# Graph network chain on Trainium2: a message gather in 128-column products, packed control words and stored one-hots

## The reference

```python
# message network, 3 layers
m = concatenate([x[src], x[dst], ew], -1)            # 103125 edges x (64 + 64 + 1)
m = relu(m @ edge_W[l] + edge_b[l])
agg = segment_sum(m, dst, n)
x = relu(concatenate([x, agg], -1) @ node_W[l] + node_b[l])
# relation network
h0 = relu(x @ W_enc + b_enc)
agg = segment_sum(einsum('nd,rdo->rno', h0, W_rel)[etypes, src], dst, n)
# sage network, 2 passes
agg = segment_sum(h[src], dst, n) / max(deg, 1)
# attention network, 2 layers: edge softmax over 2 heads, 3 power steps each
```

## Time and profile before

| what | value |
|---|---|
| median of 3 runs | 13450.17 us (13437.72 to 13457.99) |
| the profiled execution, from its first to its last instruction | 13453.0 us |
| message layer 0 | 843 us |
| message layers 1 and 2, each | 779 us |
| relation pass | 1215 us |
| sage passes | 561 and 562 us |
| attention network, from the end of the sage passes on | about 6310 us |
| TensorE busy over the whole span | 83% |
| VectorE busy over the whole span | 81% |

### The profile page before, as it was taken

The page is one execution under the profiler, slowest core; times in us unless marked ns, Lnnn a source line. Parts: engine busy times, 40 slices in busy tenths (PEclk is TensorE's granted clock), DMA queues, the critical chain, the costliest instruction groups (busy, mean ns, idle before and its releaser), DMA issues. The chain is left out here.

```text
span 13453.0 us, 456368 instructions
## 1 busy us (share of the span) xinstructions
PE 11137.4 (83%) x106911; PEld 9882.7 (73%) x106912; DVE 10911.2 (81%) x40164; ACT 5227.5 (39%) x19100; POOL 2409.1 (18%) x7659
## 2 busy tenths in 40 slices
PE   3555399899899599976665879999998789999998
PEld 3444388799798499975553339999997338999998
DVE  6545399688688288876565999999997999999998
ACT  1000022122222022235452338865453337875454
POOL 2777300000000000001110001112221001222222
PEclk9999999899899599999896999999998999999999
DMA  1111177444243011113231554432221554432222
GB/s 54 47 50 47 45 228 236 138 128 128 80 128 115 4 41 41 41 50 88 71 87 51 148 140 115 115 92 73 70 73 47 143 147 113 115 98 73 70 73 61
DMA packets 1206840, 1232.94 MB, mean 92 GB/s; under 512 B 218352, under 2 KB 1042801, under 8 KB 1206107
## 3 DMA queue, kind: packets, MB, share of 16 engines
q1 hardware_dynamic: 1180954, 1228.47, 32.8%
q0 software_dynamic: 25792, 3.35, 0.2%
HBM read 1115.06 MB, written 116.16 MB: 92 GB/s over the span
## 5 line engine op out<-in xcount | busy, mean ns | idle before, releaser
L993 DVE TENSOR_SCALAR hot<-iota_row,place 128x128 f32<-128x128 f16 (+1 forms) x9000 | 1818.8, 269 | 158.5 <-PE acc L1092 135.7
L1711 ACT ACTIVATE msgs<-G,share 128x64 f32<-128x64 f32 x6000 | 1395.6, 315 | 1346.0 <-PE G L1725 1346.0
L985 DVE TENSOR_SCALAR hotT<-idx,iota_col 128x512 bf16<-128x512 f16 x4500 | 1323.8, 352 | 524.4 <-PE G L1138 492.1
L1725 PE MATMUL G<-u_b,hotT 128*128 x12000 | 1592.2, 276 | 50.3 <-DVE hotT L1659 50.3
L1735 PE MATMUL S<-msgs,hot 128*128 128x128 f32 x12000 | 1586.3, 275 | 0.0
L1157 ACT CAST msgs<-G 128x384 bf16<-128x384 f32 x2250 | 1020.4, 480 | 1372.7 <-PE G L1138 1368.1
L1725 PEld LDWEIGHTS G<-u_b,hotT 128*128 128x128 f32 x12000 | 1467.4, 193 | 51.0 <-issue 51.0
L1735 PEld LDWEIGHTS S<-msgs,hot 128*128 128x128 f32 x12000 | 1462.3, 192 | 0.0
L1080 PE MATMUL G<-table_m,hotT 128*128 x9000 | 1309.8, 248 | 93.4 <-issue 69.3
L1110 ACT ACTIVATE msgs<-sums 128x128 f32<-128x128 f32 x2250 | 699.3, 311 | 1762.3 <-DVE sums L1102 1400.5
L1547 ACT ACTIVATE msgs<-G,msgs 128x64 f32<-128x64 f32 x6000 | 1315.5, 333 | 30.5 <-issue 21.0
(11 more groups left out here) (323 smaller groups left out, 19877.9 us busy)
## 6 DMA issues: line engine op xcount, KB each, us to landing
idx<-pos_rows SPq DMA_DIRECT2D x6375, 128.0 KB, 2.9
hotT<-hots_d SPq DMA_DIRECT2D x750, 256.0 KB
hots_d<-hotT SPq DMA_DIRECT2D x375, 256.0 KB, 3.4
key_b<-key_rows SPq DMA_DIRECT2D x62, 416.0 KB
ty_b<-type_rows SPq DMA_DIRECT2D x62, 416.0 KB
rows<-rel_rows SPq DMA_DIRECT2D x1500, 6.0 KB
ew_now<-ew_rows_d SPq DMA_DIRECT2D x1125, 3.0 KB
sorted_d<-recs,place POOLq DMA_INDIRECT x806
```

What stands on the lines that cost most here:

```text
L985: op = eng.tensor_scalar(hotT[:, c % deep, n], idx[:, c, r], p.col[:, first:first + 1], None, ALU.is_equal)
L993: op = eng.tensor_scalar(hot[:, c % 2, q], p.row16[:], place[:, c % 2, q:q + 1], None, ALU.is_equal)
L1711: op = eng.activation(msgs[:, c % 2, 2 + j // HEADS, j % HEADS * D:(j % HEADS + 1) * D], G[c % 2][1][:, j * D:(j + 1) * D], ACT.Copy, scal ...
L1725: mm = eng.matmul(G[c % 2][b][:, k * W:(k + 1) * W], hotT[:, c % 2, q * P:(q + 1) * P], table[:, ds(dst_at(at, q, 24 * W), W)], start=True ...
```

## The change

**Message layers.** The tables have four planes of 25 x 64 columns (high, middle, zeros, low part), and one product reads two planes: 128 columns as 2 x 64. For each chunk the sender and the receiver take two products each, planes 0 and 1 and then 2 and 3, into the same 128 PSUM columns, and the edge weight takes one of 64 columns with nine rows instead of three. ACT copies one of the two halves (`half`), DVE adds the other (`add`), ACT takes the relu, and DVE and POOL work out what is left over after the upper 16 bits of each message (`remains`, `lowest`). The scatter has three bf16 products of 64 columns for each chunk that read the upper halves of those fp32 values; the degree takes a product of 2 columns in layer 0. TensorE gathers quarter t and scatters quarter t-3.

**Words.** One word for each quarter holds the source block and four destination blocks of 5 bits. TensorE loads 8 to 11 words once for every eight quarters, and takes a block from a word with a shift and a remainder.

**One-hots.** Layer 0 builds all three kinds and stores them for pairs of quarters (768 KB). Layers 1 and 2 load two kinds and build the third. The relation pass loads the scatter one-hot (built before) and builds the gather ones. The sage passes load both, and ACT and DVE share the cast. SP's loads are for two quarters each.

**Set-up.** The edge weights' rows are written out nine times instead of three.

```diff
-WIDE, FIVE = 102, 5
-LAST = 4 * 512 + 4 * WIDE
+PAIRS = (QUARTERS + 1) // 2
+KINDS = 3
+LAST = (BLK - 1) * D
...
-                for i in range(EW):
+                for i in range(EW_ROWS):
...
+                chain(eng, v, [lambda: eng.tensor_copy(upper[0:1], four[:, :, 3:4])]
+                      + [lambda c=c: eng.scalar_tensor_tensor(upper[0:1], upper[0:1], 32.0, four[:, :, c:c + 1], ALU.mult, ALU.add)
+                         for c in (2, 1, 0)]
+                      + [lambda: eng.tensor_copy(one, upper[0:1]),
+                         lambda: eng.tensor_copy(upper_i[0:1], lead),
+                         lambda: eng.tensor_scalar(upper_i[0:1], upper_i[0:1], 20, None, ALU.logical_shift_left),
+                         lambda: eng.tensor_tensor(one, one, upper_i[0:1], ALU.bitwise_or)])
...
+def load_packed(p, eng, t, count):
+
+    of = p.ctl[0:1, ds(t, count)]
+    _, words = p.nc.values_load_multi_w_load_instructions(
+        of, [eng.engine], min_val=0, max_val=WORD,
+        skip_runtime_bounds_check_because="the table is computed here from block numbers that are clamped to 0..24")
+    return words
+
+
+def dst_block(word, q, times=D):
+
+    return (((word >> 5 * q) if q else word) % 32 * times).with_bounds(min_val=0, max_val=(BLK - 1) * times)
+
+
+def src_block(word, times=D):
+
+    return ((word >> 20) * times).with_bounds(min_val=0, max_val=(BLK - 1) * times)
+
...
+def tensor_turns(p, eng, step, lag):
+
+
+    words = load_packed(p, eng, 0, 8)
+    for t in range(8):
+        step(t, t, words[t], words[t - lag] if t >= lag else None)
+    with eng.Fori(1, QUARTERS // 8) as i:
+        words = load_packed(p, eng, i * 8 - lag, 8 + lag)
+        for c in range(8):
+            step(i * 8 + c, c, words[c + lag], words[c])
...
+                def lowest(t, c):
+                    ready(eng, lefted, t + 1)
+                    eng.tensor_tensor(msgs[:, c % 4, 2], msgs[:, c % 4, 1], upper[:, c % 4, 1], ALU.subtract
+                                      ).then_inc(made.h, 1)
...
+                def add(t, c):
+                    ready(eng, halved, t + 1)
+                    ready(eng, relud, t + 1)
+                    eng.tensor_tensor(sums[:, c % 4], both(c)[:, :, 0], half[:, c % 4], ALU.add).then_inc(added.h, 1)
+
+                def remains(t, c):
+                    ready(eng, relud, t + 5)
+                    eng.tensor_tensor(msgs[:, c % 4, 1], msgs[:, c % 4, 0], upper[:, c % 4, 0], ALU.subtract
+                                      ).then_inc(lefted.h, 1)
...
+                    if not make:
+                        eng.dma_start(hots[:, c:c + n, 0:2].rearrange("p k n e -> p k (n e)"),
+                                      s.hots_d[ds(pair, 1), :, 0:n, 0:2 * 4 * P].rearrange("o p k e -> (o p) k e")
+                                      ).then_inc(idx_in[c // 2].h, 16)
...
+                def gather(t, c, at):
+                    ready(eng, turned, t + 1)
+                    ready(eng, added, t - 3)
+                    of = src_block(at)
+                    for q in range(4):
+                        to = G[c % 4][:, q * 2 * D:(q + 1) * 2 * D]
+                        for side in range(2):
+                            hot = hots[:, c, 1 + side, q * P:(q + 1) * P]
+                            table = s.table3[side][:, :, ds(dst_block(at, q) if side else of, D)]
+                            eng.matmul(to.rearrange("p (i f) -> p i f", f=D), hot, table[:, 0:2],
+                                       start=(side == 0), stop=False, skip_group_check=True)
+                            eng.matmul(to.rearrange("p (i f) -> p i f", f=D), hot, table[:, 2:4],
+                                       start=False, stop=False, skip_group_check=True)
+                        mm = eng.matmul(to[:, 0:D], s.ew_now[:, c, q * P:(q + 1) * P], s.we9[:, l], start=False, stop=True,
+                                        skip_group_check=True)
+                    mm.then_inc(gathered.h, 1)
+
+                def scatter(t, c, was):
+                    ready(eng, made, t + LAG + 1)
+                    for q in range(4):
+                        hot = hots[:, c, 0, q * P:(q + 1) * P]
+                        if degrees:
+                            eng.matmul(acc[:, BLK * D:BLK * (D + 2)][:, ds(dst_block(was, q, 2), 2)],
+                                       hot, p.onesb[:], start=False, stop=False, skip_group_check=True)
+                        to = acc[:, ds(dst_block(was, q), D)]
+                        for part in range(3):
+                            mm = eng.matmul(to, hot, upper[:, c % 4, part, q], start=False, stop=False, skip_group_check=True)
+                    mm.then_inc(scattered.h, 1)
...
+                def gather(t, c, h, at):
+                    of = src_block(at)
+                    for k in range(2):
+                        q = 2 * h + k
+                        for r in range(NT):
+                            mm = eng.matmul(G[c % 2 * 2 + h][:, k * 3 * D:(k + 1) * 3 * D].rearrange("p (q f) -> p q f", f=D),
+                                            hotT[:, c % DEEP, r, q * P:(q + 1) * P] if make else hot[:, c, 1, q * P:(q + 1) * P],
+                                            tables[r][:, :, ds(of, D)], start=(r == 0), stop=(r == NT - 1))
+                    mm.then_inc(gathered[h].h, 1)
+
+                def scatter(t, c, h, was):
+                    for k in range(2):
+                        q = 2 * h + k
+                        to = acc[:, ds(dst_block(was, q), D)]
+                        for part in range(3):
+                            mm = eng.matmul(to, hot[:, c, 0, q * P:(q + 1) * P],
+                                            msgs[:, c % 4, q, part], start=False, stop=False, skip_group_check=True)
+                    return mm
...
-        def gather(eng, c, h, at, env):
-            for k in range(2):
-                q = 2 * h + k
-                for side in range(2):
-                    mm = eng.matmul(env["G"][h][:, k * 3 * D:(k + 1) * 3 * D],
-                                    env["hotT"][:, c % env["deep"], side, q * P:(q + 1) * P],
-                                    s.table3[side][:, ds(dst_at(at, q, LAST) * 2 if side else src_at(at, 24 * 3 * D), 3 * D)],
-                                    start=(side == 0), stop=False)
-                mm = eng.matmul(env["G"][h][:, k * 3 * D:(k + 1) * 3 * D], s.ew_now[:, c, q * P:(q + 1) * P],
-                                s.we3[:, l].rearrange("p q f -> p (q f)"), start=False, stop=True)
-            return mm
-
-        def scatter(eng, c, h, at, env):
-            j = (2 * (c - 1) + h) % 4
-            for k in range(2):
-                q = 2 * h + k
-                mm = eng.matmul(env["acc"][:, ds(dst_at(at, q, LAST), WIDE)], env["hot"][:, (c - 1) % 2, q, :], msgs[:, j, k, :],
-                                start=False, stop=False, skip_group_check=True)
-            return mm
...
-        s.table3 = [p.sb("table_m0", [P, BLK * 3 * D], BF16, ctx), p.sb("table_m1", [P, 2 * FIVE * 512], BF16, ctx)]
+        s.table3 = [p.sb(f"table_m{i}", [P, 4, BLK * D], BF16, ctx) for i in range(2)]
...
-        s.hots_d = p.dram("hots_d", [QUARTERS, P, 2 * 4 * P], BF16)
-        s.ew_rows = p.dram("ew_rows_d", [EW, CHUNKS * P], BF16)
+        s.hots_d = p.dram("hots_d", [PAIRS, P, 2, KINDS * 4 * P], BF16)
+        s.ew_rows = p.dram("ew_rows_d", [EW_ROWS, CHUNKS * P], BF16)
```

More of the change, by code:

```diff
@@ L33 @@
 EW = 3
+EW_ROWS = EW * EW
 RELS, RELS_BIG, HEADS, LAYERS = 8, 500, 2, 2
@@ new lines, in eights, with first_uses, ready, quarters_in @@
+def eights(eng, step):
+    for t in range(8):
+        step(t, t, t // 2)
+    with eng.Fori(1, QUARTERS // 8) as i:
+        for c in range(8):
+            step(i * 8 + c, c, i * 4 + c // 2)
+    for t in range(QUARTERS // 8 * 8, QUARTERS):
+        step(t, t % 8, t // 2)
+def first_uses(t, c, each):
+    return each * (t // 8) if isinstance(t, int) else (t - c) * (each // 8)
+def ready(eng, sem, count):
+    if not isinstance(count, int) or count > 0:
+        after(eng, sem, count)
+def quarters_in(t):
+    return 1 if isinstance(t, int) and t == QUARTERS - 1 else 2
@@ L963, in _, with store @@
-                quarters(eng, step)
-                if keep == "store":
-                    for t in range(Q - 4, Q):
-                        store(t, t % 4)
-                    for c in range(4):
-                        eng.wait_ge(stored[c].h, 16 * ((Q - c + 3) // 4))
+                def store(t, c, pair, n):
+                    ready(eng, made, t + n + LAG)
+                    eng.dma_start(s.hots_d[ds(pair, 1), :, 0:n].rearrange("o p k e -> p (o k e)"),
+                                  hots[:, c:c + n].rearrange("p k n e -> p (k n e)")).then_inc(stored[c // 2].h, 16)
@@ L970, in _ @@
+                eights(eng, step)
+                if make:
+                    for t in range((Q - 1) // 2 * 2 - 2, Q, 2):
+                        store(t, t % 8, t // 2, quarters_in(t))
```

(37 more changed lines are left out.)

424 lines of the change are left out of this document (209 added, 215 removed).

## The result

The changed kernel takes 15044.12 us in the median of 4 runs (15036.43 to 15063.28), the kernel before 13452.14; the ratio is 1.119 with an interval of 1.117 to 1.120. It is slower, as forecast, but by 1592 us where 778 were forecast, and outside the range (13,940 to 14,510). The profiled execution has a span of 15049.6 us.

What follows compares the result with a forecast made beforehand. TensorE's queue of address entries, word loads and products was taken as the bound. Layer 0 +427, layers 1 and 2 +576, relation -75, sage -160 and set-up +10 sum to +778: 14,230 us, range 13,940 to 14,510.

Steps and rivals of the forecast that it cites:

- The queue as the bound: TensorE's queue of addresses, word loads and products bounds message layers 1 and 2: 2.85 us a quarter against 2.08.
- the factor: Queue sums are multiplied by 1.025, from a sage quarter before: sum 1.46 us, measured 1.50.
- Scatter: 100+78 and 3 x 210: 808: Message layers 1 and 2: the scatter's four address entries with their products take 808 ns of queue a quarter.
- Shift and remainder: Address entries on TensorE's queue: both surcharges count in full, so an entry with both takes 132 ns.
- Rival C: Address entries: the shift is free beside the remainder, six entries at 98 ns; 13,920 us, chance 0.06.
- The load of words: TensorE's queue, once in eight quarters: 11 words take 788 ns, about 830 with what stands behind.
- the ring: Layer 0, not forecast: a store's wait on SP's queue holds back the next loads; two quarters take 9 us.
- Layer 0's stores: Layer 0: stores grow from 256 to 384 KB a quarter, but the DMAs' share, 0.61, stays hidden.
- Relation and sage: Cheaper word loads, and in sage a shorter queue, give back 75 us in relation and 80 in each sage pass.
- A: Message layers: the array bounds, not the queue, so layers 1 and 2 take 1.40 us a quarter; 12,550 us, chance 0.08.
- B: Address entries: shift and remainder cost nothing beyond a plain entry, 0.65 us less a quarter; 13,230 us, chance 0.03.
- D: Message layers: waits between engines add 1.11 times to the queue sum again, +280 us; 14,510 us, chance 0.13.

Runs made afterwards that it cites:

- aligned words: Changed kernel with each load of packed words starting four words before the group and taking 12 words; 14540.45 us, 1.087 of the kernel before.
- remainder only: On the kernel with both repairs, blocks are remainders by 25, 24, 23 and 22 of the word, without a shift; 13958.83 us, 1.037 of the kernel before.
- both repairs: Changed kernel with the aligned 12-word load and layer 0's store one pair of quarters later; 14137.25 us, 1.057 of the kernel before.
- late store: Changed kernel with only layer 0's store of the one-hots issued one pair of quarters later; 14665.78 us, 1.097 of the kernel before.
- one address a side: On the kernel with both repairs, the gather goes back to one product of 192 columns a side; 13545.48 us, 1.006 of the kernel before.
- shared addresses: On the kernel with both repairs, all four chunks of a quarter use the first one's destination block; 13050.41 us, 0.975 of the kernel before.

## Why the prediction was wrong in size, and where its mechanism held

**The queue as the bound** held. Edits that touch TensorE's entries and loads alone moved layer 1 by what they took off the queue: 83 us of queue for 82 of pass (aligned words) and 73.0 for 73.1 (remainder only). The size of the sum held in part by luck. Its 2.78 us a quarter, 2.85 with the factor, is 2.71 in the kernel with both repairs, but the term "Scatter: 100+78 and 3 x 210: 808" holds in three of eight quarters only. In the other five the entries are plain and the same rule gives 2 x 42 + 2 x 37 + 4 x 78 = 470 ns, so the mean is 597, 0.21 us less, 79 us a pass. The sum would have been 2.57, and the measured time 1.05 times that; a term too dear and a factor too small met halfway.

**Shift and remainder**: 132 taken for both in one entry, 131 to 141 measured in the gather and a median of 126 in sage; a remainder alone 88 to 94. So the surcharges do add up. Rival C (the shift free) would have been 98.

**The load of words** is the first step that failed: "11 words (593-334 is 65 for a word, so 593 + 3 x 65 = 788, about 830 with what stands behind)". It took 2637 ns. All loads of the kernel before start at a multiple of four words and take a multiple of four, and I carried their price over to one that starts three or two words ahead of such a place. By 2637, 2402 and 850 ns for 11 and 10 words off it and 12 on it, a word costs about 235 there and 65 here; 11 words on it, at 1326, lie between. It took 82 us in each of layers 1 and 2 and 84 in layer 0 (1367 to 1283, once the ring was gone), 115 in the relation pass and 84 and 87 in sage: 534 us, which turned +778 into about +1312 and the gains of the relation and sage passes into losses.

In layer 0 the load has a second price that I can't explain. The kernel with the late store and the one with both repairs, in layer 0:

```profile
L897 PEldq TENSOR_LOAD <-ctl x46: 3591/3843/4160, 1640.2 to 2952.7; - x46
```

```profile
L897 PEldq TENSOR_LOAD <-ctl x45: 857/2030/2369, 1639.3 to 2842.3; - x45
```

That is 1.2 us more than the same loads take in layer 1, 55 us over the pass, and part of why layer 0 comes to 1283 although its scatter was taken too dear as well (1336 ns a quarter, where the trace's entries and the same rule give 1155). Nearly all of these loads stand 1.4 to 1.6 us behind the issue of a store; in the kernel with one address a side they stand 3.6 to 4.1 us behind it and take 850 ns. But the kernel with the late store has one 7.4 us behind, at 3862 ns, so the place alone doesn't explain it, and no run tests a cause.

**Layer 0's stores** are the second step that failed: "0.73 x 640/512 x 2.25/3.39 is 0.61, so they hide". The bytes did hide; the wait ahead of them did not. I costed the store as traffic and never asked what stands behind its wait on SP's queue. Undone, layer 0 fell by 411 us with the load aligned (1694 to 1283), and by 323 without. The two misses together are 853 us by the passes and 832 by the ratios (1.119 to 1.057); the forecast missed by 814.

**The array** at 128 columns was taken at 56 ns, halfway between two rows, and the timeline of the kernel with shared addresses, where no queue holds it up, shows that:

```profile
3000.30 0.22 PE L1146 MATMUL G<-table_m,hots 128*128 x1
3000.30 0.10 PEld L1148 LDWEIGHTS G<-table_m,hots 128*128 128x128 bf16 x1
3000.36 0.22 PE L1148 MATMUL G<-table_m,hots 128*128 x1
...
3001.31 0.52 PE L1163 MATMUL acc<-msgs,hots 128*128 128x64 bf16 x12
```

Between 3000.30 and 3001.31 lies the gather of one quarter, 16 products of 128 columns and four of 64: 1.01 us, and 16 x 56 + 4 x 29 is 1.01. The Trainium skill's 81 ns for a sustained pair of weight load and product at 128 columns ("TensorE: Matmul & The Clock Gate", "Back-to-back issue gap") is not what this kernel shows; the formula of the same section, 56 ns, which it gives for a single product, fits.

**Hidden work**: POOL's subtraction, given 0.3 to 1.4 us, took 0.615; DVE's additions, 0.35 to 0.52, took 0.42. Both were hidden; DVE in layer 0, given 55 to 65% of the span, has 38% in the kernel after and 53% with both repairs (677 of 1270 us). **Relation and sage** would have gained what was forecast within 31 and 20 us, once the load was aligned. **Set-up**: layer 0 starts at 1688 us before and 1692 after, where 10 more were forecast, but this stretch differs by more between the groups of runs, so that term is open.

**The rivals**: A's mechanism failed, and its price too: with nine of fourteen entries gone the message layers stop at 1.95 us a quarter, at loads. B and C are refuted by the entries' durations, 131 to 141 ns where B had 48 and C 98. D, slower still by 280 us, had the side of the miss but a third of its size, and named neither cause.

## What to carry to other kernels

Price an instruction from a row with the same alignment as well as the same size: a load into registers that started off a 16-byte place cost more than three times as much for each word, and 11 words cost more than 12 from the same kind of start. Read the queue's entries in every step of an unrolled loop, since some of them may be worked out already. When a store joins a queue that also issues loads, ask what its wait waits for and whether that needs the loads behind it; put it behind them and give it a longer lag. Count the addresses before splitting a product: each half asked for one more, and here the halves cost more than they gained.

## What the runs showed of the hardware

- A load of words into TensorE's registers took about 335 ns for 4, 600 for 8, 850 for 12 and 1360 for 20 words that start at a multiple of four words, 1326 for 11 from such a start, and 2402 for 10 and 2637 for 11 from another. In layer 0 with the late store the same loads took 1.2 us more; why is open.
- An address entry on TensorE's queue took 37 to 51 ns plain, 88 to 94 with a remainder, 123 to 141 with shift and remainder. In message layer 1, 73 us less of entries made the pass 73 us shorter.
- Addresses that are equal are worked out once: nine of fourteen entries a quarter went when the four chunks shared a block. The scatter's entries were plain in five of eight quarters, which fits the same.
- The granted clock followed the waiting: 0.68 in layer 0 while the array stood idle for several us in each pair of quarters, 0.88 with the ring undone, 0.99 in layer 1 with shared addresses.
